# Edge attention over a large node table: an inside sort, gathers by rank, and rows kept on chip

## The reference

```python
dst, src = (edge_index[0], edge_index[1])
edge_feat = jnp.concatenate([h[dst], h[src], rel_pos, distance], axis=-1)
x = jax.nn.silu(edge_feat @ W1 + b1)
x = jax.nn.silu(x @ W2 + b2)
scores = (x @ W3 + b3)[:, 0]
mx = jax.ops.segment_max(scores, dst, num_segments=num_nodes)
exp_scores = jnp.exp(scores - mx[dst])
den = jax.ops.segment_sum(exp_scores, dst, num_segments=num_nodes)
alpha = exp_scores / (den[dst] + EPS)
msg = h[src] @ Wv * (alpha * node_weight[src])[:, None]
out = jax.ops.segment_sum(msg, dst, num_segments=num_nodes)
return h + out
```

## Time and profile before

| what | us |
|---|---|
| median of 3 runs | 1216.1 |
| lowest, highest | 1198.22, 1221.03 |
| the profiled execution | 1221.44 |
| its span, first to last instruction | 1219.7 |
| PE, DVE, ACT, POOL busy | 908.1, 873.2, 478.0, 772.8 |

### The profile page before, as it was taken

The page is one execution under the profiler, slowest core; times in us unless marked ns, Lnnn a source line. Parts: engine busy times, 40 slices in busy tenths (PEclk is TensorE's granted clock), DMA queues, the critical chain, the costliest instruction groups (busy, mean ns, idle before and its releaser), DMA issues.

```text
span 1219.7 us, 17877 instructions
## 1 busy us (share of the span) xinstructions
PE 908.1 (74%) x3370; PEld 545.7 (45%) x3395; DVE 873.2 (72%) x4138; ACT 478.0 (39%) x1030; POOL 772.8 (63%) x788
## 2 busy tenths in 40 slices
PE   0008589999999999999994777776776777687770
PEld 0004345555555554555543454454545444455440
DVE  7988567767667666767652578877786887877884
ACT  0004466656666666666652122222222221222221
POOL 4502476667667677667601447777777777777775
PEclk9997778668768787768765878878787787877785
DMA  5301798999999999999973223333233232223321
GB/s 159 98 0 22 221 309 253 276 307 281 270 292 299 283 306 300 267 300 302 271 234 135 77 66 85 83 86 82 79 84 80 84 85 79 81 81 84 82 63 35
DMA packets 103676, 200.71 MB, mean 165 GB/s; under 512 B 17166, under 2 KB 75092, under 8 KB 91104
## 3 DMA queue, kind: packets, MB, share of 16 engines
q1 hardware_dynamic: 75424, 137.29, 37.6%
q0 software_dynamic: 28224, 63.13, 19.5%
HBM read 111.53 MB, written 90.27 MB: 165 GB/s over the span
## 4 chain that ended last, share of the span: by engine, by line
PE 30%; DVE 23%; issue 18%; POOL 12%; DMA 10%; ACT 4%; SPq 1%; DVEq 0%; POOLq 0%; ACTq 0%
DMA back<-in_xw,gidx 7%; POOL out_rows L370 5%; POOL back L358 5%; PE p_dt L512 3%; PE p L476 3%; PE p L477 3%; PE p L478 3%; PE p_m L482 3%; PE p L536 3%; DVE shared L843 3%; ACT xout L401 3%; PE p L487 3%; PE p_w L493 2%; DVE shared L609 2%; PE p_hT L469 2%
## 5 line engine op out<-in xcount | busy, mean ns | idle before, releaser
L401 ACT ACTIVATE xout<-xin,rs 128x128 f32<-128x128 f32 x637 | 259.7, 482 | 174.7 <-DVE rs L732 58.3
L326 POOL DMA_INDIRECT hs<-in_xw,gidx x196 | 185.4, 946 | 182.5 <-DVE gidx L588 99.4
L358 POOL DMA_INDIRECT back<-rec_d,ridx x196 | 206.8, 1055 | 136.9 <-issue 63.7
L370 POOL DMA_INDIRECT out_rows<-res,sidx x196 | 195.0, 995 | 61.4 <-issue 55.7
L326 POOL DMA_INDIRECT back<-in_xw,gidx x196 | 185.5, 946 | 59.8 <-issue 55.2
L755 DVE BATCH_NORM_STATS2 st<-xin 128x6 f32<-128x128 f32 x784 | 217.5, 285 | 0.1
L431 ACT ACTIVATE shared<-p_dt 128x1024 f32<-128x1024 f32 x49 | 50.2, 1024 | 336.9 <-PE p_dt L530 336.9
L777 DVE SCALAR_TENSOR_TENSOR x<-th,p 128x512 f32<-128x512 f32 x49 | 33.7, 688 | 168.0 <-PE p L488 104.8
L536 PE MATMUL p<-ones,shared 1*128 1x1 f32 x392 | 60.9, 272 | 95.3 <-DVE x L865 95.3
L536 PEld LDWEIGHTS p<-ones,shared 1*128 1x128 f32 x392 | 57.0, 219 | 137.2 <-DVE x L865 111.5
L437 ACT ACTIVATE res<-x,rs 128x128 f32<-128x128 f32 x196 | 80.7, 482 | 83.6 <-DVE rs L732 81.0
(11 more groups left out here) (132 smaller groups left out, 1773.5 us busy)
## 6 DMA issues: line engine op xcount, KB each, us to landing
xin<-in_xw SPq DMA_DIRECT2D x49, 1032.0 KB, 7.5
out_rows<-xout SPq DMA_DIRECT2D x49, 1024.0 KB
rec_d<-rec SPq DMA_DIRECT2D x49, 258.0 KB, 12.9
rec_d<-back SPq DMA_DIRECT2D x49, 256.0 KB, 12.3
far<-far_d SPq DMA_DIRECT2D x49, 128.0 KB, 3.1
hs<-in_xw,gidx POOLq DMA_INDIRECT x196
back<-in_xw,gidx POOLq DMA_INDIRECT x196
back<-rec_d,ridx POOLq DMA_INDIRECT x196, 2.8
```

The lines of the kernel that those rows point to most:

```text
L326: pool.indirect_dma_start(out=to(q), out_offset=None, in_=xw, in_offset=bass.IndirectOffsetOnAxis(ap=index(q), axis=0)).then_inc(sems[r], 16)
L358: pool.indirect_dma_start(out=back[:, r, q, :], out_offset=None, in_=rec_d, in_offset=bass.IndirectOffsetOnAxis(ap=ridx[:, r, q:q + 1], ax ...
L370: pool.indirect_dma_start(out=out, out_offset=bass.IndirectOffsetOnAxis(ap=sidx[:, r, q:q + 1], axis=0), in_=res[:, r, q, :], in_offset=No ...
L401: ins = nc.scalar.activation(xout[:, t.slot(d, XO), j, :], xin[:, t.slot(d), j, 0:H], ACT.Identity, bias=rs[:, t.slot(d, 2), 1, j:j + 1], ...
```

## The change

The kernel is written anew around the same tiles. In words:

- First half, the senders only (50 turns). POOL gathers sender rows in original order (`hs`, six slots) as soon as the sender numbers are loaded. One product per tile with the two matrices side by side gives the sender's part of the first layer and half the message; the four edge features come in through a bf16 matrix of 36 rows (three parts each, split at the start). A record is 256 numbers, three slots. The sort is a generator, and a few steps are taken per turn: 8 in each of the first two, then 3. It ends in turn 42 with index tables in the SBUF. 16 dense blocks, one in three turns.
- Second half, the receivers (64 steps). POOL gathers receiver rows by rank (`hk`, all 49 groups have their own place on chip) and records by rank (`r`, twelve slots). Both layers, scores, and a softmax for four groups at once on 16 partitions of 128 columns. The sum over edges of a receiver is now a product with a 128x128 matrix of weights per tile, built on DVE. Sums that go over a tile's border are put right at the end with two extra scatters. The other 33 dense blocks run in the first 37 of these steps.
- POOL's order is one list: 49 hs; 8 hk; 41 pairs of r and hk; 8 pairs of r and sc (scatter of a group); 41 sc; the two extra scatters. Before every second group, up to the last 20, there is a memset of a 128x512 tile (`idle`) and a wait for its end, 87 in all.
- Silu replaces Tanh and the multiply after it; the root's chain has 13 steps; one statistics instruction does two rows.

Its core:

```diff
-RING = 4
+HS_RING, EF_RING, REC_RING, R_RING, X_RING = 6, 4, 3, 12, 4
+HK_SEMS, SC_SEMS, Y_SEMS, FAR_RING = 16, 8, 4, 4
+Z_LAG, M_LAG = 9, 8
+SORT_FIRST, SORT_EACH = 8, 3
+LEAD = 8
+REST = 20
+B0 = G + 1
...
+def dense_plan():
+    first = [1 + 3 * j for j in range(16)]
+    return first + [B0 + (k * 9) // 8 for k in range(NB - len(first))]
...
+            pool.wait_ge(S["snd_in"], 16)
+            plan = pool_plan()
+            for n, (kind, g) in enumerate(plan):
+                if n % 2 == 0 and 0 < n < len(plan) - REST:
+                    nc.gpsimd.memset(idle[:], 0.0).then_inc(S["idled"], 1)
+                    pool.wait_ge(S["idled"], n // 2)
+                if kind == "hs":
+                    wait(pool, "rec23", g - HS_RING + 1)
+                    wait(pool, "rec01", g - HS_RING + 1)
+                    for q in range(TPG):
+                        t = g * TPG + q
+                        gather(hs[:, g % HS_RING, q, :], xw, snd_t[:, t:t + 1], hs_in[g % HS_RING])
+                elif kind == "hk":
+                    if g == 0:
+                        pool.wait_ge(S["tab_ready"], 1)
...
+                elif kind == "r":
+                    if g == 0:
+                        for r in range(REC_RING):
+                            pool.wait_ge(rec_out[r], 16 * len(range(r, G, REC_RING)))
+                        pool.wait_ge(S["rows_out"], 64)
+                    wait(pool, "z_ready", g - R_RING + 1)
...
+                else:
+                    if g == 0:
+                        pool.wait_ge(S["dense_written"], 1)
+                    wait(pool, "res_ready", g + 1)
...
+            for i in range(B0):
+                steps = SORT_PLAN[i] if i < len(SORT_PLAN) else 0
+                dense_norm(i)
+                dense_stats(i)
+                for n in range(steps):
...
+                    next(network, None)
+                    more(2)
+                if i >= 1:
...
+                    vec.tensor_copy(rec[:, j % REC_RING, 2:4, 0:H], pair(j, 2)[:, :, 0:H])
+                    ins = vec.tensor_tensor(rec[:, j % REC_RING, 2:4, H:RW], pair(j, 2)[:, :, H:RW], w, ALU.mult)
...
+                    ins = vec.tensor_scalar(m_q[:, g % 2, q, :], bank[4][:, q * P:(q + 1) * P], kcol[:, t:t + 1],
+                                            acol[:, b % 2, n:n + 1], ALU.is_equal, ALU.mult)
...
+                vec.tensor_tensor(flat, bank[5 + g % 2][:], flat, ALU.add).then_inc(S["y_done"], 1)
...
+                if 0 <= s - 2 < G:
+                    nc.scalar.activation(x2[:], bank[2][:], ACT.Silu, bias=bcol[:, 1:2]).then_inc(S["x2_ready"], 1)
+                norm(B0 + s, 4, 8)
+                if 0 <= s - 1 < G:
+                    nc.scalar.activation(x1[:], bank[1][:], ACT.Silu, bias=bcol[:, 0:1]).then_inc(S["x1_ready"], 1)
+                for b in range(NBATCH):
+                    if batch_end(b) + 4 == s:
+                        nc.scalar.activation(soft[0:n, 3, :], soft[0:n, 2, :], ACT.Exp).then_inc(S["p_ready"], 1)
...
+                    for q in range(TPG):
+                        ins = pe.matmul(bank[5 + g % 2][:, q * P:(q + 1) * P], m_q[:, g % 2, q, :], rr[:, g % R_RING, q, H:RW],
+                                        start=True, stop=True)
```

More of the change, by code:

```diff
@@ L160, in gnn_kernel @@
[L160 to L168, removed]
@@ L189, in wait @@
[L189 to L204, removed]
-            with eng.Fori(1, ROUNDS - 2) as k:
-                for u in range(RING):
-                    body(Turn(k, u))
-            for k in (ROUNDS - 2, ROUNDS - 1):
-                for u in range(RING):
-                    body(Turn(k, u))
-            for u in range(extra):
-                body(Turn(ROUNDS, u))
@@ L214, in column @@
-        def column(table, g, fixed):
-            return table[:, g * TPG:(g + 1) * TPG] if fixed else table[:, bass.ds(g * TPG, TPG)]
+        row = {n: part(SORTW) for n in ("key", "id", "next", "neg", "mul", "start", "sidx", "kg", "pos", "seg", "zero")}
+        row_i = part(SORTW).bitcast(I32)
+        far16 = part(SORTW // 2).bitcast(BF16)
+        cont16 = part(SORTW // 2).bitcast(BF16)
+        edge = part(32)
+        assert at[0] <= R_RING * TPG * RW, at[0]
+        hflat = hk[:].rearrange("p g q h -> p (g q h)")
@@ new lines, in gnn_kernel, with wait, wait_ring, pair @@
+        scattered = [sem(f"scattered{r}") for r in range(SC_SEMS)]
+        block = ctx.enter_context(nc.Block())
+        def wait(eng, s, n):
+            if n > 0:
+                eng.wait_ge(S[s], n)
+        def wait_ring(eng, ring, i, per):
+            if i >= 0:
+                eng.wait_ge(ring[i % len(ring)], (i // len(ring) + 1) * per)
+        def pair(j, q):
+            return bank[2 + 2 * (j % 2) + q // 2][:].rearrange("p (two w) -> p two w", two=2)
+        def blocks(u):
+            return [j for j in range(NB) if DSTEP[j] == u]
@@ L306, in _ @@
[L306 to L319 removed]
+            sp.wait_ge(S["consts"], 1)
@@ L879, in _, with more, dense_stats, gate @@
-            rounds(dve, body2, 1)
+                after(12)
+                step(vec.scalar_tensor_tensor(out=bi, in0=s[:, :, 1], scalar=-1.0, in1=r, op0=ALU.mult, op1=ALU.mult)); yield
+            running = []
+            def more(n=1):
+                while n and running:
+                    if next(running[0], "over") == "over":
+                        running.pop(0)
+                    else:
+                        n -= 1
+            def dense_stats(u):
+                for j in blocks(u):
+                    wait_ring(dve, x_in, j, 16)
+                    for n in range(0, BR, 2):
+                        ins = vec.bn_stats(dst[:, n:n + 2, :].rearrange("p j w -> p (j w)"),
+                                           xin[:, j % X_RING, n:n + 2, :].rearrange("p j h -> p h j"))
+                        more()
+                    ins.then_inc(S["dstats"], 1)
+                    more(99)
+                    def gate():
+                        wait(dve, "norm_a", j - 1)
+                    running.append(chain(("dstats", j + 1), BR, dst, drs[:, j % 2], cwd, "chain_d", j * STEPS, gate))
@@ new lines, in dense_norm @@
+            def dense_norm(u):
+                for j in blocks(u - 1):
+                    wait(dve, "chain_d", (j + 1) * STEPS)
+                    for n in range(ACT_ROWS, BR):
+                        ins = vec.tensor_scalar(xin[:, j % X_RING, n, :], xin[:, j % X_RING, n, :],
+                                                drs[:, j % 2, 0, n:n + 1], drs[:, j % 2, 1, n:n + 1], ALU.mult, ALU.add)
+                        more()
+                    ins.then_inc(S["norm_d"], 1)
+            network = sort()
```

1361 lines of the change are left out of this document (733 added, 628 removed).

## The result

The changed kernel takes 1068.6 us in the median (1065.9 to 1069.9, four runs), the kernel before in the same comparison 1218.6 (1198.2 to 1227.9). The ratio is 0.885, 95% interval 0.873 to 0.897: faster by 11.5%. Forecast was 1088, with a range of 1045 to 1158.

A forecast was written before the change was run, and what follows sets the result against it. The prediction took POOL's cadence of 1.25 to 1.35 us per indirect transfer as the floor. Its terms, 3.5 + 986 + 70 + 5 + 16 + 6 = 1086.5 us, and 1.7 around them gave 1088, range 1045 to 1158.

The forecast's parts named there:

- Start: Kernel start: POOL waits only for the first load of sender numbers, 3.5 us where it was 12 before.
- Transfers: Whole POOL list: 588 gathers at 1.25 us and 198 scatters at 0.97 + 0.30, 986 us in sum.
- Fills: 87 POOL memsets of 128x512 in POOL's list: 0.5 us plus one gap of 0.3 each, 70 us in all.
- Allowance for order in the pairs: Receiver half, 41 pairs of r and hk groups: 0.4 us a step lost to order, 16 us in all.
- First sc: Start of the scatters: the first one waits for the last dense store, 5 us, bounds 0 and 15.
- End: Kernel end: the last transfer starts 6 us before the span's end, kept at 6 us.
- The sums for the other engines: Work of DVE, ACT, PE and DMA per turn or step, all put below POOL's pace in both halves.
- (B): Receiver half: the loop of waits between engines sets the pace, 12.5 us a step, 53 more: 1141 us; chance 0.17.
- (C): Sender half: its record writes set the pace, a turn of 6.5 us, 54 more: 1142 us; chance 0.08.
- (E): Receiver half: pairs take 14.8 us with PE at 1.2 GHz, 148 more: 1236 us; chance 0.08.
- (D): Whole kernel: a fill is 0.1 us long and engine order costs nothing, 1011 to 1045 us; chance 0.05.
- The 59 us: Sender half: upper bound if each gather met a sort instruction of about 0.3 us that held it off.

The follow-up runs named there:

- the added scans: 60 DVE scans of 512 columns put behind DVE's last step of the changed kernel: 1067.9 us with both inputs in SBUF, 1064.6 with the second in PSUM.

## Why the prediction was right

Its range and sign hold, and its mechanism, POOL's cadence of 1.25 us per transfer as the floor, is what the trace shows in every slice. 1086.5 us was its sum for the span; it is 1064.0. Term by term, in its order:

- Start: 3.5 forecast, 3.05 measured.
- Transfers: 986 forecast. POOL's list from 3.05 to its end at 1055.6 is 1052.6 us; less the fills (69 x 0.51 + 18 x 1.07 = 54) it is 998. 7 to 8 of the 12 us more are in the sender half: 3.5 us of waits and a mean of 965 instead of 946 ns, the three gathers held by casts included. The rest is about a hundredth of a us per transfer. That the sort costs POOL next to nothing was right, but not that each transfer is spared: where two or three of its instructions followed on one another, a gather took up to 1.23 us (at 196.48, until 0.83 after the second of them).
- Fills: 70 forecast, 54 measured. The length was right (0.5, measured 0.546), the gap was not: a fill needs no gap of its own, so 0.51 and not 0.8 ahead of gathers; ahead of scatters 1.07, which no row had shown. The 0.8 taken for all was too much for 69 fills and too little for 18.
- Allowance for order in the pairs: 16 forecast, none measured. POOL waited 0.9 us for PE's products in the whole kernel. The working took the 4% by which a turn of before exceeded PE's busy time and put it on top of POOL. But an engine whose work does not depend on the loop, with eleven slots ahead of it, does not take part in the loop's losses until the loop is slower than itself, and that loop runs at 9.6 us (the run without receiver gathers). This is the term that was wrong in kind.
- First sc: 5 forecast, none measured; with POOL relieved the wait was 10.3, so it is real and was covered here.
- End: 6 forecast, 8.4 measured (the last transfer starts at 1054.67 and takes 0.97).

The differences, -0.5 + 12 - 16 - 16 - 5 + 2.4, make -23, which takes 1086.5 to about 1064. Terms that were too small by 14 us hid part of the 37 us by which others were too large; to that extent the closeness of the number is luck.

The sums for the other engines, per step of the pairs: DVE 7.9 forecast and 7.3 measured (294 us over 40.6 steps), ACT 7.9 to 8.5 and 7.4, PE 7.4 and 6.5, at a clock of 0.80 where 0.73 was taken. Table loads: 24 of 1.28 us came with Silu and Exp, 31 us on ACT and none on the path, as allowed for. Per turn of the sender half: DVE 4.2 and 4.3, ACT 3.4 and 2.9, PE 4.0 and 4.7. Two were clearly off. PE in the sender half: 2.9 us at full clock would be 3.7 at the 0.78 that was granted, and 4.7 were measured. DMA in the pairs: 9.1 forecast (9.2 with the 1.86 MB of dense data that 8/9 of a block are, not 1.82), 0.66 x 10.5 = 7.0 measured. The queues from 312 to 740 us after (packets, MB, share):

```profile
q1 hardware_dynamic: 9632, 65.22, 40.9%
q0 software_dynamic: 13004, 31.99, 24.9%
```

65.22 MB in 0.409 x 428 us are 373 GB/s, where the earlier trace rows had 300. A packet has 6.8 KB on average now, 2.0 KB then: the table without its 129th column and no record writes between. But the size of the packets is not the reason by itself. In the sender half after, from 0 to 268 us, it was 1.8 KB, and the rate 58.16 MB in 0.610 x 268 us, 356 GB/s:

```profile
q1 hardware_dynamic: 33162, 58.16, 61.0%
```

The 300 of before were read where the DMA engines were busy 0.99 of the time. The estimate took that rate over to stages that load them less; what sets the rate is open.

The rivals: (B), a loop of 12.5 us, falls with 9.6 measured. Its picture of unequal steps in each four was right (the gaps of 7.7 and 2.9 us), but its mean was not. (C) did not come: records land 6.7 us after issue instead of 13.0, and SP's writes held nobody. (E) needed PE at 1.2 GHz throughout; it had 0.80. (D) needed a fill of 0.1 us. Of what the prediction said would show it right, the first gather (3.5, 3.05), the end of the sender half (268, 267.8) and the first r (312, 309.9) came out within 3 us. The first sc came 32 us earlier (780, 748.1), which is the allowance, the 0.3 us of each of 41 fills and the 5 us for the last store. The scatters alone took 220 us where 215 were forecast, for their dearer fills. The rule of the Trainium skill (SBUF — State Buffer, Who interferes with whom) that the prediction weighed, that the ports which the two engines share are taken as an exclusive lock, fits the 32 held transfers of before and the five held scatters. The 59 us by which the working bounded it, 0.3 for every gather, were far too high: all gathers of the sender half together were 4 us longer than at 946 ns. A held transfer ends 0.75 to 0.83 us after the DVE instruction, and one that is free takes 0.95, so the first 0.1 to 0.2 us behind its start are free in any case.

What it did not see is how close behind the sender half was. It gave PE 4.0, DVE 4.2 and DMA 5.1 us of 5.4 and concluded that POOL paces by little; with the fills in, that was true by a hair. But it was not a busy time that came next. Without the fills DVE's wait for a load that was issued two turns ahead decided, and behind that its wait for PE.

## What to carry to other kernels

Count the indirect transfers and multiply them by their full cadence, busy time and gap; a queue that shows 75% busy can be 100% taken. Here, once that queue had work from the first microsecond to the last, only what was in its own list counted, and a wait elsewhere mattered only where it was longer than what the ring held. When its own list is shortened, look again at the stage with the least room: there the gain stops, and what stopped it here was a load issued two turns ahead.

## What the runs showed of the hardware

- An indirect DMA on POOL takes 0.95 us for 128 rows, of 512, 516 or 1024 bytes alike (949, 946 to 965, 952 ns), and a scatter 0.97 to 0.98; the next one starts 0.30 us after.
- A memset behind one starts with no gap, and is followed by 0.27 us to the next gather, but by 0.79 to 1.10 to the next scatter. Without fills a group of scatters starts 0.30 after the last.
- A transfer that starts 0.07 us or more after a DVE scan with two SBUF inputs, and before its end, ends no sooner than 0.75 to 0.81 us after that scan (32 of before, 5 of the added ones); after a long cast it is 0.81 to 0.82. One that starts before the scan, or at most 0.05 us after it began, is not held. With one input in PSUM none was held, 45 of before and 41 beside the added scans.
- Plain DMA moved, in its busy share of the time, 373 GB/s with packets of 6.8 KB, 356 with 1.8 KB, and 300 with 2.0 KB where the engines were busy 0.99 of the time.
